# Attention stage of a decoder layer: score pieces of heads 0 and 1 made ahead, and later keys hidden on GpSimd after the exponential

## The chip, the core and the metric

The kernel runs on one NeuronCore of a Trainium2 chip. Its engines are TensorE (PE in the rows; PEld is its weight load), VectorE (DVE), ScalarE (ACT), GpSimd (POOL) and SyncE (SP, which issues DMAs). Each works through its own instructions in order and waits on semaphores for the others. The metric is the device time of one execution in microseconds (us); lower is better.

## What is computed

A decoder layer for 2048 tokens of 256 features: causal self-attention with 16 heads of 16 features, a second mixing step against a context of 1601 rows, and a feed-forward step with 8 experts, two of which are chosen for each token. The change touches the first of them, which the reference writes as

```
scores = jnp.einsum('bhqd,bhkd->bhqk', q, k) / jnp.sqrt(jnp.float32(Dh))
causal = jnp.tril(jnp.ones((S, S), dtype=bool))
scores = jnp.where(causal[None, None], scores, jnp.float32(-jnp.inf))
attn = jax.nn.softmax(scores, axis=-1)
out = jnp.einsum('bhqk,bhkd->bhqd', attn, v)
```

## The kernel before, in words

Three functions run one after the other: `project` (queries, keys, values, and the matrix of the second step), `attend` (the 16 heads) and `finish` (output products, second step, feed-forward step).

**Each head is computed twice over, in two layouts.** The softmax needs each query's highest score. So the scores are first made with the queries on the partitions, only to find their maximum: 35 **pieces** for a head (`PIECES`), most 512 columns wide. A piece is one product of `qstack` and `kstack` (`form_piece`, L154), and where it crosses the causal diagonal two more products with the matrix `hide_keys` (L161), which add -1e30 to later keys. VectorE takes a piece's maximum into `partial` (`reduce_piece`, L172). The letters of the pieces: w is 512 columns below the diagonal, d is 512 columns at it, n is 384 at it, p two of 256 and q four of 128. When all 35 are in, VectorE makes `neg_max` (L850), TensorE turns it (L807, the entry "max"), VectorE writes `max_row` (L855), and SP copies it by two DMAs into a row of `qstack` (L666), so that the scores of the second layout come out with the maximum taken off.

**The second layout** has the keys on the partitions, and goes by 10 **quads** for a head (`QUADS`): 512 queries against four tiles of 128 keys. Quads 0, 2, 5 and 9 of a head lie at the diagonal. For a quad `scores_half` makes two banks of scores (L747), ScalarE takes the exponential of each (L709) into one of three buffers `probs`, and `weigh` multiplies them by the values into `acc` (L774), two quads later (`LAG`). At the diagonal a score tile gets two more products, with `hide_queries` (L756), 64 and 128 columns wide, which again add -1e30. ScalarE copies `acc` out for each block of queries (L714), and the sums are folded (L782, "fold") and turned (L789, "turn").

**What sets the order.** TensorE's order in `attend` is a table, `PLACES`: for each of a head's 10 quads what goes behind the first half of the scores, behind the second half, and behind the weighing. What stands there are pieces of later heads and the entries fold, turn and max; they pass through a ring of three PSUM banks, which VectorE empties in the same order. During head h TensorE makes the pieces of head h+1 in quads 0 to 5 and those of head h+2 in quads 6 to 9: 35 in each of heads 0 to 13, 20 in head 14, none in head 15. In `project` another table (`pieces_behind`) puts pieces in pairs behind other products: all 35 of head 0 and the 15 early ones of head 1, 50 in all. `project` has three stretches that matter here: "v" (L552, 16 steps), "t" (L565, 13 steps) and "m" (L574, 26 steps).

**GpSimd** in `attend` prepares the weights of the third step: for each head it scales a load (L684), casts it (L687) and makes the rest (L689), all three in a row, after the load has landed. SP issues the max rows, the stacks of a head four ahead (12 DMAs), the store of the split weights and the next load, in this order.

## Time and profile before

| | us |
|---|---|
| Median of 3 runs | 839.01 (837.18 to 839.31) |
| The profiled execution, its own time | 840.59 |
| Its span, first to last instruction | 838.9 |
| `project`, from the start of the span to about | 88 |
| `attend`, about | 88 to 470 |
| `finish` | the rest |

| Engine | busy, us | share of the span |
|---|---|---|
| TensorE | 783.6 | 93% |
| VectorE | 559.2 | 67% |
| ScalarE | 512.3 | 61% |
| GpSimd | 303.8 | 36% |

The shares are averages over stages with different limits. In `attend`, VectorE is at nine tenths or more of nearly every slice, and falls to a third in `finish`. TensorE's granted clock is full nearly everywhere. Matmul ends are modelled, so for TensorE starts are a better measure than durations.

### The profile page before, as it was taken

To read this page: it belongs to the slowest core of one execution; us is meant where nothing else is said; L and a number is where in the kernel's file an instruction comes from. 1 tells how busy PE (TensorE), PEld (TensorE's weight loads), DVE (VectorE), ACT (ScalarE), POOL (GpSimd) and SP (SyncE) were. 2 spreads that over 40 slices of the span, in tenths; PEclk is the share of its full clock that TensorE was granted. 3 is DMA by queue.
4 is the path that set the end of the run, shared out by engine and by line. 5 is a ranking of instruction groups with operands and counts; after the bars stand their busy time and mean duration, and the time that the engine had idled before them with its cause. 6 is when DMAs were issued, how large, how long until landed. Compare 5 with 4: busy or idle time off the path is not lost. (4 is left out here: it accounts for less than half of the span.)

```text
span 838.9 us, 19596 instructions
## 1 busy us (share of the span) xinstructions
PE 783.6 (93%) x7434; PEld 496.9 (59%) x7435; DVE 559.2 (67%) x1072; ACT 512.3 (61%) x756; POOL 303.8 (36%) x226
## 2 busy tenths in 40 slices
PE   5899899999999999999998797889999999999994
PEld 1367344444443444444433585778888888877883
DVE  4575699999999999999980496973333333222395
ACT  4441687778887877788879487254444444343543
POOL 5040595555333355554550112132333333301121
PEclk9999799999999999999999999999999999999998
DMA  8783343334444443334232598452222222221362
GB/s 295 131 214 152 113 152 108 103 123 133 143 151 152 152 132 109 105 133 139 106 115 114 209 398 214 150 190 65 77 75 75 75 75 75 76 58 52 102 195 76
DMA packets 68362, 111.47 MB, mean 133 GB/s; under 512 B 39485, under 2 KB 49918, under 8 KB 63934
## 3 DMA queue, kind: packets, MB, share of 16 engines
q1 hardware_dynamic: 63134, 93.36, 35.7%
q0 software_dynamic: 4816, 16.65, 6.0%
q10 hardware_dynamic: 336, 0.40, 0.4%
q8 instruction: 54, 0.88, 0.4%
q14 instruction: 22, 0.18, 0.1%
HBM read 66.60 MB, written 32.37 MB: 118 GB/s over the span
## 5 line engine op out<-in xcount | busy, mean ns | idle before, releaser
L172 DVE TENSOR_REDUCE partial<-ring 128x1 f32<-128x512 f32 (+3 forms) x510 | 312.8, 670 | 24.2 <-PE ring L154 18.8
L709 ACT ACTIVATE probs<-scores 128x1024 f32<-128x1024 f32 (+1 forms) x320 | 270.5, 902 | 69.6 <-PE scores L747 36.9
L1284 ACT ACTIVATE hid<-turned 128x512 f32<-128x512 f32 (+1 forms) x112 | 65.6, 586 | 160.7 <-PE turned L1445 130.9
L154 PE MATMUL ring<-kstack,qstack 48*128 48x512 f16 (+1 forms) x581 | 156.4, 354 | 2.4 <-DVE partial L172 0.2
L774 PE MATMUL acc<-probs,values 128*32 128x512 f32 (+2 forms) x1472 | 156.6, 496 | 0.5 <-ACT acc_sb L714 0.3
L1470 PE MATMUL ops<-weights,work 128*128 (+1 forms) x1320 | 148.9, 273 | 2.7 <-DVE work L1685 1.4
L1445 PE MATMUL turned<-mats,weights 128*128 128x256 f16 (+1 forms) x1344 | 143.6, 262 | 3.2 <-DMA mats<-attn 2.2
L747 PE MATMUL scores<-qstack,kstack 49*128 49x512 f16 (+3 forms) x640 | 135.1, 352 | 7.2 <-ACT probs L709 5.9
L1685 DVE TENSOR_TENSOR work<-hid,work 128x512 f16<-128x512 f32 (+1 forms) x112 | 76.8, 690 | 94.9 <-ACT work L1289 94.8
L1470 PEld LDWEIGHTS ops<-weights,work 128*128 128x128 f16 x1320 | 128.4, 98 | 18.9 <-issue 3.8
L684 POOL TENSOR_TENSOR a_w_in<-a_w_in,w_scale 128x2304 f32<-128x2304 f32 x16 | 64.4, 4027 | 202.6 <-DMA a_w_in<-w_all 202.6
L1445 PEld LDWEIGHTS turned<-mats,weights 128*128 (+1 forms) x1344 | 122.2, 98 | 21.4 <-issue 4.4
L154 PEld LDWEIGHTS ring<-kstack,qstack 48*128 48x128 f16 x581 | 45.3, 94 | 116.5 <-DVE partial L172 101.5
L1209 POOL DMA_INDIRECT by_token<-attn,dest_u x39 | 38.7, 991 | 143.9 <-DVE attn L1694 138.1
L689 POOL TENSOR_TENSOR a_w_out<-a_w_in,a_w_out 128x2304 f16<-128x2304 f32 x16 | 73.0, 4566 | 1.3
L1289 ACT ACTIVATE work<-hid 128x512 f16<-128x512 f32 (+1 forms) x112 | 69.7, 622 | 4.7
L774 PEld LDWEIGHTS acc<-probs,values 128*32 128x32 f32 x1472 | 43.7, 109 | 36.8 <-issue 26.6
L747 PEld LDWEIGHTS scores<-qstack,kstack 49*128 49x128 f16 x640 | 40.6, 94 | 37.7 <-ACT probs L709 28.9
L1694 DVE COPY attn<-ops 128x512 f32<-128x512 f32 (+1 forms) x20 | 13.6, 678 | 68.8 <-PE ops L1470 68.8
L161 PEld LDWEIGHTS ring<-hide_keys,ident 64*128 64x128 bf16 x460 | 41.3, 95 | 17.3 <-issue 0.6
L161 PE MATMUL ring<-hide_keys,ident 64*128 64x128 bf16 x460 | 51.2, 203 | 0.0
L1201 POOL DMA_INDIRECT attn<-rows_d,token_u x39 | 38.1, 976 | 30.3 <-issue 10.7
(203 smaller groups left out, 742.5 us busy)
## 6 DMA issues: line engine op xcount, KB each, us to landing
a_w_in<-w_all SPq DMA_DIRECT2D x16, 1152.0 KB, 9.1
w_split_d<-a_w_out SPq DMA_DIRECT2D x16, 1152.0 KB, 5.7
weights<-w_split_d SPq DMA_DIRECT2D x6, 2048.0 KB, 19.8
weights<-w_split_d POOLq DMA_DIRECT2D x3, 2048.0 KB, 12.1
qstack<-q_split SPq DMA_DIRECT2D x72, 64.0 KB, 2.7
kstack<-k_split SPq DMA_DIRECT2D x72, 64.0 KB, 2.8
weights<-by_token SPq DMA_DIRECT2D x8, 512.0 KB, 7.6
attn<-xT SPq DMA_DIRECT2D x4, 512.0 KB, 7.4
```

Source lines behind the costliest of these rows:

```text
L154: mm = nc.tensor.matmul(bank[:, at:at + w], qstack[rows, slot, t * P:(t + 1) * P], kstack[rows, slot, c:c + w], start=True, stop=not diagonal)
L161: mm = nc.tensor.matmul(bank[:, at - P + a:at - P + b], ident16[rows, copy], hide_keys[rows, copy, a:b], start=False, stop=part == 1)
L172: return nc.vector.tensor_reduce(out=found[:, places[0]:places[-1] + 1:step], in_=bank[:, 0:WIDTH[n]].rearrange("p (k w) -> p k w", k=len( ...
L689: nc.gpsimd.tensor_tensor(w_out[:, h % 2, 1], w_in[:, h % 2], w_out[:, h % 2, 0], ALU.subtract).then_inc(w_lo, 1)
L709: nc.scalar.activation(probs[:, quad % NPROBS, at:at + w], scores[half][:, first:first + w], ACT.Exp, scale=QK_SCALE).then_inc(exp_done, 1)
L747: mm = nc.tensor.matmul(scores[half][:, at:at + w], kstack[used, slot, kt * P:(kt + 1) * P], qstack[used, slot, (qb + 1) * QB - w:(qb + 1) ...
L774: mm = nc.tensor.matmul(acc[VW * group:VW * (group + 1), first_query:first_query + w], values[:, h, k0 + j], probs[:, quad % NPROBS, at:at ...
L1284: nc.scalar.activation(h32, hps[b].rearrange("p (j n) -> p j n", n=TW)[:, :, 0:w], ACT.Silu, scale=1.0 / WSCALE).then_inc(silu_done, 1)
L1289: nc.scalar.activation(hid[:, parity, 0, b * HB:(b + 1) * HB, 0:w], h32, ACT.Copy).then_inc(hid_hi, 1)
L1445: mm = nc.tensor.matmul(place.rearrange("p (g n) -> p g n", n=P), weights[:, a, bass.ds(at + (k * HID + (b * HB + j) * P), P)], turned_row ...
L1470: mm = nc.tensor.matmul(bank[:, i], hid[:, parity, a, j, i * P:(i + 1) * P], weights[:, c, bass.ds(at + (WE // 2 + j * D), D)], start=(m = ...
L1685: nc.vector.tensor_tensor(hid[:, parity, 1, chunks, 0:w], hid32[:, b % 2].rearrange("p (j n) -> p j n", n=TW)[:, :, 0:w], hid[:, parity, 0 ...
```

## The change

1. **Pieces.** All 35 pieces of heads 0 and 1 are made in `project`, 70 in all, by putting a pair behind each step of "t" (before, behind two of three) and behind every second step of "m" (before, every fourth) but the last. The 490 others are dealt over `attend` by `deal_ring`, one head after the other, without regard to where a head begins: 34 in each of heads 0 to 2, 33 in each of heads 3 to 13, 25 in head 14. Within a head they stand more evenly: quad 1 and quad 8 hold one fewer than before.
2. **The entry "max"** no longer stands in quad 8, but four pieces behind the last piece of its head, so it moves from head to head: quad 1 in head 1, quad 2 in head 2, up to quad 8 in heads 12, 13 and 14. In head 13 it stands at the very end of quad 8, behind the weighing. For head 1 it is the first entry of `attend`.
3. **Later keys.** The products with `hide_queries` are gone, and so is the matrix. Instead GpSimd sets the probabilities of later keys to 0 behind the exponential: one `affine_select` for each half of a quad at the diagonal, over two blocks of 128 columns, 8 for a head. The weighing of such a quad now waits for `later_hidden`.
4. **GpSimd's weights.** The three steps for a head's weights are spread between the selects: two behind those of quad 5, and the third behind those of quad 0 of the next head.

```diff
-PLACES = (("", "wd", "w"), ("w", "w", "nw"), ("", "ww", "w"), ("d", "w", "w"), ("", "ww", "Fwp"),
-          ("", "wn", "w"), ("w", "d", "w"), ("w", "n", "w"), ("qMT", "wd", "nw"), ("", "ww", "wp"))
+ORDER = "wdwwnwqwdnwwwwpwdwwwnwwwwdwwwwwpwnw"
+PLACES = (("", "xx", "x"), ("x", "x", "x"), ("", "xx", "x"), ("x", "x", "x"), ("", "xx", "Fxx"),
+          ("", "xx", "x"), ("x", "x", "x"), ("x", "x", "x"), ("T", "xx", "xx"), ("", "xx", "xx"))
...
     if kind == "m":
-        return 2 if n % 4 == 3 else 0
-    return 2 * {"qk": n >= NQ * 4 - 2, "v": n % 2, "t": n % 3 != 2}[kind]
+        return 2 if n % 2 == 1 and n < DC * CT - 1 else 0
+    return 2 * {"qk": n >= NQ * 4 - 2, "v": n % 2, "t": 1}[kind]
...
+            def hide_later(h, qb):
+                quad = h * NQUAD + LAST_QUAD[qb]
+                for half in range(2):
+                    (_, a, _), (_, b, _) = halves_of(LAST_QUAD[qb])[half]
+                    at = half * 2 * QB + a
+                    pool.wait_ge(exp_done, 2 * quad + half + 1)
+                    blocks = probs[:, quad % NPROBS, at:at + 2 * (b - a)].rearrange("p (k n) -> p k n", k=2)[:, :, 0:P]
+                    nc.gpsimd.affine_select(out=blocks, in_=blocks, compare_op=ALU.is_ge, fill=0.0,
+                                            base=0, pattern=[[0, 2], [1, P]], channel_multiplier=-1).then_inc(later_hidden, 1)
...
             for h in range(H):
...
+                for qb in range(NQ):
+                    hide_later(h, qb)
+                    for _ in range(WEIGHTS_BEHIND[qb]):
+                        u = done // 3
+                        if done < 3 * H and (u < h or u == h and h > 0 or qb == 2):
+                            split_weights(u, done % 3)
+                            done += 1
...
-                if diagonal:
-                    for part, b in enumerate((GROUP, P)):
-                        for group, (j, at, w) in enumerate(halves_of(s)[half]):
-                            copy, used = hide_half(group, part), group_rows(group, GROUP)
-                            mm = nc.tensor.matmul(scores[half][:, at:at + b], ident16[used, copy],
-                                                  hide_queries[used, copy, 0:b], start=False, stop=part == 1)
...
             def weigh(h, s):
...
-                pe.wait_ge(exp_done, 2 * quad + 2)
                 first, last = k0 == 0, s == LAST_QUAD[qb]
+                if last:
+                    pe.wait_ge(later_hidden, 2 * (h * NQ + qb) + 2)
+                else:
+                    pe.wait_ge(exp_done, 2 * quad + 2)
```

**TensorE in `project`, the first five steps of "t".** A row is a line of the kernel, what it does, the tiles and the columns. Before:

```order
L565 MATMUL vt_ps0<-lm_sb,ctxT_sb 128x256 x2
L154 MATMUL piece_ps2<-kstack,qstack 128x512
L154 MATMUL piece_ps0<-kstack,qstack 128x512
L565 MATMUL vt_ps1<-lm_sb,ctxT_sb 128x256 x2
L154 MATMUL piece_ps1<-kstack,qstack 128x512
L154 MATMUL piece_ps2<-kstack,qstack 128x512
L565 MATMUL vt_ps0<-lm_sb,ctxT_sb 128x256 x2
L565 MATMUL vt_ps1<-lm_sb,ctxT_sb 128x256 x2
L154 MATMUL piece_ps0<-kstack,qstack 128x512
L154 MATMUL piece_ps1<-kstack,qstack 128x512
L565 MATMUL vt_ps0<-lm_sb,ctxT_sb 128x256 x2
```

And now (line 180 is the former line 154, line 585 the former 565):

```order
L585 MATMUL vt_ps0<-lm_sb,ctxT_sb 128x256 x2
L180 MATMUL piece_ps2<-kstack,qstack 128x512
L180 MATMUL piece_ps0<-kstack,qstack 128x512
L585 MATMUL vt_ps1<-lm_sb,ctxT_sb 128x256 x2
L180 MATMUL piece_ps1<-kstack,qstack 128x512
L180 MATMUL piece_ps2<-kstack,qstack 128x512
L585 MATMUL vt_ps0<-lm_sb,ctxT_sb 128x256 x2
L180 MATMUL piece_ps0<-kstack,qstack 128x512
L180 MATMUL piece_ps1<-kstack,qstack 128x512
L585 MATMUL vt_ps1<-lm_sb,ctxT_sb 128x256 x2
L180 MATMUL piece_ps2<-kstack,qstack 128x512
```

A pair now stands behind every step, where before every third step had none.

**TensorE in `attend`, a quad at the diagonal** (the last quad of the last head, which has no pieces around it). Before:

```order
L747 MATMUL scores0<-qstack,kstack 128x512
L747 MATMUL scores0<-qstack,kstack 128x128
L756 MATMUL scores0<-hide_queries,ident16 128x64 x2
L756 MATMUL scores0<-hide_queries,ident16 128x128 x2
L747 MATMUL scores1<-qstack,kstack 128x384
L747 MATMUL scores1<-qstack,kstack 128x256
L756 MATMUL scores1<-hide_queries,ident16 128x64 x2
L756 MATMUL scores1<-hide_queries,ident16 128x128 x2
L774 MATMUL acc<-probs,values 32x512 x8
```

And now:

```order
L792 MATMUL scores0<-qstack,kstack 128x512
L792 MATMUL scores0<-qstack,kstack 128x128
L792 MATMUL scores1<-qstack,kstack 128x384
L792 MATMUL scores1<-qstack,kstack 128x256
L812 MATMUL acc<-probs,values 32x512 x8
```

Eight small products have gone from the quad, and with them the place between the two halves' scores.

**GpSimd in `attend`, in the middle of the heads.** Before, the three steps for one head's weights stand in a row, and nothing lies between them:

```order
L694 TENSOR_TENSOR res<-res,bo_rows 128x1024 x4
L684 TENSOR_TENSOR a_w_in<-a_w_in,w_scale 128x2304
L687 CAST a_w_out<-a_w_in 128x2304
L689 TENSOR_TENSOR a_w_out<-a_w_in,a_w_out 128x2304
L684 TENSOR_TENSOR a_w_in<-a_w_in,w_scale 128x2304
```

And now, where `x4` are the selects of two quads:

```order
L709 AFFINE_SELECT probs<-probs 128x2x128 x4
L715 TENSOR_TENSOR a_w_in<-a_w_in,w_scale 128x2304
L721 CAST a_w_out<-a_w_in 128x2304
L709 AFFINE_SELECT probs<-probs 128x2x128 x4
L724 TENSOR_TENSOR a_w_out<-a_w_in,a_w_out 128x2304
L709 AFFINE_SELECT probs<-probs 128x2x128 x4
```

The last step (L689 before, L724 now) has moved between the selects of quad 0 and those of quad 2 of the next head.

## Rows read from the trace of the kernel before

**Rows 1.** The page's first part: busy time of each engine
```profile
PE 783.6 (93%) x7434; PEld 496.9 (59%) x7435; DVE 559.2 (67%) x1072; ACT 512.3 (61%) x756; POOL 303.8 (36%) x226
```

**Rows 2.** Windows: busy us (instructions), an ordinary head, then head 15
```profile
core 0: us, PE busy (x) PEld busy (x) DVE busy (x) ACT busy (x) POOL busy (x), PEclk, DMA share, GB/s
...
253.90:277.60 23.70, 23.35 (x256) 10.11 (x252) 22.36 (x40) 18.99 (x25) 10.59 (x4) 1.00 0.42 135
444.72:464.50 19.78, 17.58 (x187) 6.77 (x187) 0.68 (x2) 18.70 (x25) 0.00 (x0) 1.00 0.24 95
```

**Rows 3.** Timeline of VectorE in one head: start, length, what, count [idle before]
```profile
276.77 12.36 DVE L172 TENSOR_REDUCE partial<-ring 128x1 f32<-128x512 f32 x20
...
291.96 2.35 DVE L172 TENSOR_REDUCE partial<-ring 128x1 f32<-128x512 f32 x4 [0.57 <-PE ring L154]
```

**Rows 4.** Waits in one head, 270.3 to 293.95 us: total, times, longest
```profile
PEld ring L154 <- DVE partial L172: 7.0, 10, 0.8
...
DVE partial L172 <- PE ring L154: 0.9, 3, 0.6
```

**Rows 5.** TensorE's waits in head 15, 444.72 to 464.50 us
```profile
PE scores L747 <- ACT probs L709: 1.5, 5, 0.4
```

**Rows 6.** Timeline of TensorE in head 15, quads without pieces
```profile
446.38 0.64 PE L747 MATMUL scores<-qstack,kstack 49*128 49x512 f16 x4
446.94 0.75 PE L774 MATMUL acc<-probs,values 128*32 128x320 f32 x12
...
454.89 0.39 PE L747 MATMUL scores<-qstack,kstack 49*128 49x512 f16 x2
...
455.55 1.06 PE L774 MATMUL acc<-probs,values 128*32 128x512 f32 x8
```

**Rows 7.** Timeline of TensorE in the first stage, stretch "t"
```profile
53.89 1.13 PE L565 MATMUL vt_ps<-lm_sb,ctxT_sb 128*128 128x256 f32 x4
...
55.27 1.13 PE L565 MATMUL vt_ps<-lm_sb,ctxT_sb 128*128 128x256 f32 x4
...
56.94 2.00 PE L565 MATMUL vt_ps<-lm_sb,ctxT_sb 128*128 128x256 f32 x8
58.87 0.39 PE L154 MATMUL piece_ps<-kstack,qstack 48*128 48x512 f16 x2
```

**Rows 8.** The entry "max" on TensorE: shortest/median/longest ns, first and last start
```profile
L807 PE MATMUL ring<-ident,neg_max x15: 277/277/278, 109.1 to 440.5; 128*16 128x128 f32 x15
```

**Rows 9.** Windows at the start of the attention stage, columns as in rows 2
```profile
91.00:92.00 1.00, 0.82 (x11) 0.44 (x8) 1.00 (x3) 1.00 (x2) 0.00 (x0) 0.54 1.06 442
...
98.00:99.00 1.00, 1.00 (x8) 0.00 (x0) 0.00 (x0) 0.19 (x1) 1.00 (x1) 0.50 0.00 0
```

**Rows 10.** GpSimd's groups by line: count, busy us, mean ns, idle before
```profile
L443 POOL TENSOR_TENSOR values<-values,bv_rows 128x256 f32<-128x256 f32 x16 | 11.2, 721 | 29.3 <-ACT values L387 29.3
...
L420 POOL TENSOR_SCALAR_AFFINE_SELECT ident<-ident 128x128 f32<-128x128 f32 x1 | 0.3, 287 | 0.0
```

**Rows 11.** Timeline of GpSimd in one head, the longest step
```profile
276.50 4.57 POOL L689 TENSOR_TENSOR a_w_out<-a_w_in,a_w_out 128x2304 f16<-128x2304 f32 x1
```

**Rows 12.** Timeline of ScalarE: the exponentials of quads 0 and 2
```profile
280.99 1.30 ACT L709 ACTIVATE probs<-scores 128x640 f32<-128x640 f32 x2 [1.24 <-PE scores L756]
...
285.56 1.32 ACT L709 ACTIVATE probs<-scores 128x640 f32<-128x640 f32 x2
```

**Rows 13.** Timeline of TensorE: "max" turned, next head's first scores, weighing of quad 2
```profile
275.20 0.28 PE L807 MATMUL ring<-ident,neg_max 128*16 128x128 f32 x1
...
280.27 0.22 PE L747 MATMUL scores<-qstack,kstack 49*128 49x128 f16 x1
...
289.99 0.75 PE L774 MATMUL acc<-probs,values 128*32 128x320 f32 x12
```

**Rows 14.** Timeline of SyncE's queue: the DMAs of the max row are issued
```profile
276.21 1.15 SPq L666 DMA_DIRECT2D qstack<-max_row  x2
```

**Rows 15.** The tile `max_row`: from a DMA's issue to its landing
```profile
DMA to landing us min/median/max: 1.7/2.2/3.4
```

140 lines of the change are left out of this document (80 added, 60 removed).

## The prediction, made before the changed kernel ran

> **What bounds the kernel now.** I read the page's busy times first. TensorE is at 93% of the span, the others far below [rows 1], but that is an average over three stages, and the change lies in the first two. So I went on with windows. In an ordinary head of 23.7 us TensorE is busy for 23.35 us and VectorE for 22.36, ScalarE for 18.99, GpSimd for 10.59 [rows 2]. Two engines are nearly full at once, and the reader should see how they share the bound. VectorE's timeline shows 20 maxima without a gap in 12.36 us, 0.618 us each, and later short gaps that end with a piece from TensorE [rows 3]. The waits of one head say the same: VectorE waits 0.9 us for TensorE's pieces in a whole head, and TensorE's weight load for pieces is held by VectorE ten times [rows 4]. Most of that held time runs beside other products, since TensorE itself is idle for only 0.35 us. In head 15 no pieces are left. There the head takes 19.78 us, TensorE is busy for 17.58, and its stops are for ScalarE [rows 2, 5]. So pieces and masks are work on the bound in heads 0 to 14, and ScalarE sets a floor of about 19.8 us.
>
> From the two windows, a piece costs TensorE (23.35 - 17.58) / 35 = 0.165 us in `attend`, because it fills the idle row group beside the scores, and it costs VectorE 0.618 us.
>
> **Twenty pieces into the first stage.** They go as ten pairs. A step of "t" with its pair takes 55.27 - 53.89 = 1.38 us from start to start, and two steps without a pair between them 58.87 - 56.94 = 1.93, that is 0.97 for one [rows 7]. So a pair costs 0.41 us there, more than twice 0.165, since it stands alone between full-array products. Ten pairs are 4.1 us. Of the 20 pieces, 15 are w, 2 d, 2 n and 1 p, so six places at the diagonal come with them; each mask is 192 columns, which at the rate of the plain pair (512 columns in each of two row groups in about 0.3 us) is near 0.1 us: 0.6 us more. Sum 4.7 us, all on the path, because TensorE is what ends in this stretch. VectorE needs 2 x 0.618 = 1.24 us for a pair and has 1.38, so it keeps up, with 0.14 us to spare in each step. If that cover is gone, each step costs what VectorE lacks.
>
> **Fewer and more even pieces in the heads.** VectorE's part of a head with 35 pieces is 35 x 0.618 = 21.6 us and 1.1 us for the reciprocal, the product, the row and the last maximum: 22.7, and the rest to 23.7 is 1.0 us of gaps. With 33 pieces it is 20.4 + 1.1 + 1.0 = 22.5; with 34, 23.1.
>
> **The masks of the scores.** They are 16 x 4 x 8 = 512 small products. A quad at the diagonal without pieces takes 455.55 - 454.89 = 0.66 us with its masks, and a whole quad, which has more columns of scores (1024 against 896 in the fuller row group), 446.94 - 446.38 = 0.56 us [rows 6]. So the masks cost at least 0.10 us a quad, 0.4 a head. From above: they also keep the second row group idle until the first has finished, and pieces could fill that; 0.25 us a quad, 1.0 a head, is the most that I find in the columns. I take 0.7, since most quads have pieces to put there. TensorE's part of a head with 33 pieces is then 17.58 - 0.7 + 33 x 0.165 = 22.3 us and 0.35 idle: 22.65. Both engines come out within 0.15 us of each other, and I take 22.6: **1.1 us less** for each of heads 3 to 13. With 34 pieces VectorE sets 23.1, 0.6 less for each of heads 0 to 2. Head 15 is set by ScalarE and gains nothing. Head 14 has 5 pieces more than before (0.8 us of TensorE) and no masks (0.7): nothing.
>
> **The selects on GpSimd.** They lie between an exponential and the weighing, so what hides them is the two quads of lag. The trace has one select of 128 columns of f32 at 0.287 us; a sum of two tensors of 256 columns takes 0.721 us [rows 10]. The new one has 256 columns and one input, so 0.29 is its lower bound and 0.72 its upper, and I take 0.45, nearer to the row of its own kind. The tightest place is quad 2, since the longest step for the weights, 4.57 us [rows 11], now stands before it. The exponential of quad 0 ends at 280.99 + 1.30 = 282.29, and the weighing of quad 2 starts at 289.99 [rows 12, 13]: 7.7 us, and 7.3 when the head is 5% shorter. In this time GpSimd does a select, the long step and two selects: 4.57 + 3 x 0.45 = 5.9 us, and 6.7 at the upper bound. It fits with 1.4 us to spare, so I cost the selects at nothing. Queued behind a late select would be the other weight steps, and for it waits TensorE's weighing, with everything behind that. The three steps are also late in their turn by a few us, which only SP's store waits for, and that DMA has no reader before the last stage. The page gives GpSimd 36% [rows 1], so 128 selects of 0.45 us are no load.
>
> The Trainium skill, GPSIMD Engine Reference, section 3.1, states that data-dependent branching costs about 12 cycles an element; if a select were such work, 256 elements would be an estimated 2.6 us each by that page, and the sum would turn to slower, as in the second rival below. By that rule the 128 columns in rows 10 would have taken about 1.3 us; the trace has 0.287 and doesn't agree, so the sum goes by the row.
>
> **The entry "max".** In most heads it comes earlier than before and nobody waits for it. Before, TensorE turned it at 275.20 and needed the row at 280.27, 5.1 us later [rows 13]; SP issued the DMAs at 276.21 and they land about 2.2 us after the issue of the second, near 279 [rows 14, 15]. For head 14 it now stands behind the weighing of quad 8, about 2.4 us ahead of head 14's first scores (two pieces, then quad 9). The chain needs about 3.4 us there, as VectorE has little queued. So head 14 starts **1.0 us** late.
>
> **The sum.** -3 x 0.6 - 11 x 1.1 + 1.0 + 4.7 = -8.2 us. The profiled execution took 840.59 us for a span of 838.9, 1.6 us above the median of 839.01. I take the difference from the median: 830.8 us.
>
> **The rivals.**
>
> *More from the masks.* If they hold up the pairing of row groups in nearly every quad at the diagonal, and VectorE's gaps shrink with the more even table, a head gains 1.6 us: -3 x 1.2 - 11 x 1.6 + 5.7 = -15.5, 823.5 us. For it: eight products stand between the halves. Against it: VectorE at 21.5 us without gaps leaves little more.
>
> *Slower: selects that TensorE waits for.* One mechanism: at quad 2 of heads 3 to 15, GpSimd must finish the 4.57 us step and three selects in 7.3 us. It decides from (7.3 - 4.57) / 3 = 0.91 us a select. At 1.5 us each the weighing is 1.8 us late in each of 13 heads: +23 us, 854 us. Against it are both rows of rows 10; for it, that no row shows this form (two blocks, in place) and that spans on GpSimd are rough.
>
> *The gain meets another bound.* ScalarE has 18.99 us of 23.7 and no slack from quad 2 to quad 5, where copies lie between its exponentials. If heads gain only 0.4 us: -14 x 0.4 + 5.7 = +0.1, so 839 us, no change. VectorE's evenness argues against it.
>
> *The clock.* In head 0 TensorE's granted clock is at half (1.2 GHz of 2.4) from about 91.5 us on, after a stop between the two stages [rows 9]. From the first entry "max", at 109.1 us, to the one in rows 13 are seven heads, 23.7 us each [rows 8, 13]: so head 0 is the one that lost, about 2 to 3 us. If more pieces in "m" keep the clock up, the time is 828; if a stretch at half clock falls elsewhere, 834. This moves the forecast and turns no sign.
>
> *It doesn't do what it says.* The number of pieces is 560 in both tables, so 20 are moved and none saved; the masks of the pieces (L161) stay. That is as costed.
>
> **Chances.** The forecast with either clock (826 to 836) 0.60; more from the masks 0.15; another bound, no change 0.14; selects waited for 0.07; others that make it slower, such as VectorE falling behind in the first stage by more than 0.3 us a step, 0.04. The range reaches to the rivals at 823.5 and 839 with the clock's 3 us below: 820 to 838.5. Runs of this kernel differ by about 0.3%, 2.5 us, and what lies within that of 839 counts as no change: faster is then under 836.5, and gets 0.76, no change 0.14, slower 0.10.
>
> **What the profile of the changed kernel would show.** The first stage ends about 4.7 us later, with "t" and "m" steps of 1.38 us. From entry to entry of the reciprocal, an ordinary head takes 22.6 us. Selects take 0.3 to 0.7 us, and no wait of the weighing for `probs` from GpSimd stands among the waits. TensorE stops for about 1 us before head 14. VectorE still has stretches of 20 maxima without a gap; if they are gone and TensorE has no stops, the masks were worth more than 0.7. The prediction is wrong if selects take over 0.9 us, or if ScalarE's exponentials stand without gaps through a whole head.

## The result

| | before | after |
|---|---|---|
| Median, us | 838.94 (837.18 to 839.31, 4 runs) | 846.38 (845.62 to 848.25, 4 runs) |
| The profiled execution, us | 840.59 | 846.47 |
| Its span, us | 838.9 | 844.7 |
| Ratio to before | | 1.0096, 95% interval 1.0075 to 1.0118 |

The changed kernel is 7.4 us slower. The prediction was 830.8 us, with a range of 820 to 838.5: wrong in sign, and outside the range.

**Where the time went.** The stages are cut at starts that both traces have. First the start of the scores of head 0, of before and then of after, from TensorE's timeline:

```profile
87.99 0.37 PE L747 MATMUL scores<-qstack,kstack 49*128 49x512 f16 x2 [1.09 <-PEq L267]
```
```profile
92.63 0.37 PE L792 MATMUL scores<-qstack,kstack 49*128 49x512 f16 x2 [0.94 <-PEq L292]
```

Then the reciprocals, one for each head. The first, the thirteenth and the last of before, and the same three of after, from VectorE's timelines:

```profile
133.64 0.26 DVE L836 RECIPROCAL inv<-ring 128x16 f32<-128x16 f32 x1
...
418.63 0.26 DVE L836 RECIPROCAL inv<-ring 128x16 f32<-128x16 f32 x1
...
469.34 0.26 DVE L836 RECIPROCAL inv<-ring 128x16 f32<-128x16 f32 x1 [7.61 <-PE ring L789]
```
```profile
136.94 0.26 DVE L873 RECIPROCAL inv<-ring 128x16 f32<-128x16 f32 x1
...
423.07 0.25 DVE L873 RECIPROCAL inv<-ring 128x16 f32<-128x16 f32 x1
...
474.55 0.26 DVE L873 RECIPROCAL inv<-ring 128x16 f32<-128x16 f32 x1 [7.60 <-PE ring L827]
```

Twelve ordinary heads took (418.63 - 133.64) / 12 = 23.75 us each before and (423.07 - 136.94) / 12 = 23.84 after. The forecast had them 1.1 us shorter. With the first weighings of heads 1, 14 and 15 as further cuts (119.59, 428.33 and 449.42 us before; 123.42, 432.95 and 454.74 after) the spans split so:

| Stretch | forecast, us | measured, us |
|---|---|---|
| first stage | +4.7 | +4.6 |
| head 0, from its first scores | -0.6 | -0.8 |
| heads 1 to 13 | -13.3 | +0.8 |
| head 14 | +1.0 | +0.7 |
| head 15 up to the last reciprocal | 0 | -0.1 |
| `finish` | 0 | +0.6 |
| sum (difference of the two spans) | -8.2 | +5.8 |

Nearly all of the miss lies in the ordinary heads. The term of head 14 came near its size by another mechanism (see the account of the prediction), and head 0 begins at half clock in both kernels, so its -0.8 can't be put down to the pieces alone. The medians lie 7.4 us apart, the two profiled executions 5.9: the one of before took 840.59 us against a median of 838.94.

**The page after.** The first line corresponds to [rows 1]; the two groups are the maxima of the pieces on VectorE and the pieces on TensorE (columns: busy us, mean ns, idle us just before them with what ended most of it).

```profile
PE 781.0 (92%) x6922; PEld 478.7 (57%) x6923; DVE 562.0 (67%) x1072; ACT 512.5 (61%) x756; POOL 352.0 (42%) x350
...
L198 DVE TENSOR_REDUCE partial<-ring 128x1 f32<-128x512 f32 (+3 forms) x490 | 302.3, 669 | 35.1 <-PE ring L180 19.5
...
L180 PE MATMUL ring<-kstack,qstack 48*128 48x512 f16 (+3 forms) x560 | 154.2, 355 | 9.7 <-DVE partial L198 7.2
```

The same groups of before:

```profile
L172 DVE TENSOR_REDUCE partial<-ring 128x1 f32<-128x512 f32 (+3 forms) x510 | 312.8, 670 | 24.2 <-PE ring L154 18.8
...
L154 PE MATMUL ring<-kstack,qstack 48*128 48x512 f16 (+1 forms) x581 | 156.4, 354 | 2.4 <-DVE partial L172 0.2
```

TensorE has 512 products less and VectorE 20 maxima less in the heads, and both now wait for each other: VectorE's idle time before maxima grew by 10.9 us, TensorE's before pieces by 7.3. The windows of an ordinary head and of head 15, to be read against [rows 2]:

```profile
core 0: us, PE busy (x) PEld busy (x) DVE busy (x) ACT busy (x) POOL busy (x), PEclk, DMA share, GB/s
213.80:237.60 23.80, 22.77 (x219) 8.72 (x219) 21.74 (x39) 19.55 (x26) 13.78 (x11) 1.00 0.42 136
448.00:466.80 18.80, 16.57 (x151) 5.16 (x147) 0.57 (x3) 17.85 (x25) 7.69 (x9) 1.00 0.31 127
```

TensorE's work fell by 0.6 us a head and VectorE's by 0.6 [rows 2], and the head did not get shorter. In TensorE's timeline after, the waits stand where four pieces come together (over one head's length; idle before and its releaser in brackets):

```profile
237.42 0.39 PE L180 MATMUL ring<-kstack,qstack 48*128 48x512 f16 x1 [0.31 <-DVE partial L198]
...
261.15 0.39 PE L180 MATMUL ring<-kstack,qstack 48*128 48x512 f16 x1 [0.40 <-DVE partial L198]
```

Both stand in the turn of quad 0 (turns are explained next), and another wait of 0.30 us stands at 258.66 in that of quad 9. The reader should see that TensorE stops there for VectorE, though VectorE has 2 us to spare in the head as a whole.

### The profile page after: what moved, and what is told of

The parts are those of the page before. It is cut to its first block and busy times, and to the rows that moved or that the text cites. A ratio compares the mean times of both kernels' runs of the same rounds, so it can differ in the third digit from the quotient of the medians.

```text
span 844.7 us, 18690 instructions
## 1 busy us (share of the span) xinstructions
PE 781.0 (92%) x6922; PEld 478.7 (57%) x6923; DVE 562.0 (67%) x1072; ACT 512.5 (61%) x756; POOL 352.0 (42%) x350
## 5 line engine op out<-in xcount | busy, mean ns | idle before, releaser
L198 DVE TENSOR_REDUCE partial<-ring 128x1 f32<-128x512 f32 (+3 forms) x490 | 302.3, 669 | 35.1 <-PE ring L180 19.5
L180 PE MATMUL ring<-kstack,qstack 48*128 48x512 f16 (+3 forms) x560 | 154.2, 355 | 9.7 <-DVE partial L198 7.2
L1485 PE MATMUL turned<-mats,weights 128*128 128x256 f16 (+1 forms) x1344 | 145.5, 263 | 1.0 <-issue 0.7
L792 PE MATMUL scores<-qstack,kstack 49*128 49x512 f16 (+3 forms) x640 | 129.1, 352 | 9.4 <-ACT probs L755 7.2
L709 POOL TENSOR_SCALAR_AFFINE_SELECT probs<-probs 128x256 f32<-128x256 f32 x128 | 51.3, 407 | 184.4 <-ACT probs L755 184.4
L180 PEld LDWEIGHTS ring<-kstack,qstack 48*128 48x128 f16 x560 | 42.4, 94 | 128.0 <-DVE partial L198 111.4
L724 POOL TENSOR_TENSOR a_w_out<-a_w_in,a_w_out 128x2304 f16<-128x2304 f32 x16 | 73.1, 4567 | 0.1
L792 PEld LDWEIGHTS scores<-qstack,kstack 49*128 49x128 f16 x640 | 37.3, 94 | 41.6 <-ACT probs L755 31.2
```

Source lines behind the costliest of these rows:

```text
L180: mm = nc.tensor.matmul(bank[:, at:at + w], qstack[rows, slot, t * P:(t + 1) * P], kstack[rows, slot, c:c + w], start=True, stop=not diagonal)
L198: return nc.vector.tensor_reduce(out=found[:, places[0]:places[-1] + 1:step], in_=bank[:, 0:WIDTH[n]].rearrange("p (k w) -> p k w", k=len( ...
L724: nc.gpsimd.tensor_tensor(w_out[:, u % 2, 1], w_in[:, u % 2], w_out[:, u % 2, 0], ALU.subtract).then_inc(w_lo, 1)
L792: nc.tensor.matmul(scores[half][:, at:at + w], kstack[used, slot, kt * P:(kt + 1) * P], qstack[used, slot, (qb + 1) * QB - w:(qb + 1) * QB ...
L1485: mm = nc.tensor.matmul(place.rearrange("p (g n) -> p g n", n=P), weights[:, a, bass.ds(at + (k * HID + (b * HB + j) * P), P)], turned_row ...
```

## How the experiments are read: turns

The head's time is cut into ten **turns**. A turn of quad s runs from one weighing on TensorE to the next, and holds what stands behind the weighing in quad s - 1 and then both halves of quad s. Starts of weighings are read from TensorE's timeline; in all kernels but the changed one and its kin each head repeats them to 0.01 us. Pieces are counted from the table. Each ratio below is taken against the kernel before measured beside the run (medians 838.8 to 840.1 us). (The recorded expectations count quads from one: their "first quad" is quad 0, their "fourth" quad 3, their "seventh" quad 6, their "ninth" quad 8.)

| Turn of quad | 3 | 4 | 5 | 6 | 7 | 8 | 9 | 0 | 1 | 2 | head |
|---|---|---|---|---|---|---|---|---|---|---|---|
| pieces before | 3 | 3 | 4 | 3 | 3 | 4 | 4 | 4 | 3 | 4 | 35 |
| before | 2.04 | 2.11 | 3.07 | 2.27 | 2.01 | 3.07 | 2.39 | 2.58 | 1.97 | 2.25 | 23.75 |
| select_only | 2.04 | 2.11 | 3.06 | 2.28 | 2.01 | 3.06 | 2.39 | 2.58 | 1.97 | 2.25 | 23.75 |
| before_cheap | 2.04 | 2.12 | 2.85 | 2.27 | 2.01 | 2.88 | 2.19 | 2.36 | 1.97 | 2.25 | 22.94 |
| select_cheap | 2.04 | 2.12 | 2.85 | 2.28 | 2.00 | 2.88 | 2.19 | 2.31 | 1.97 | 2.25 | 22.89 |
| drop_bound | 2.04 | 2.11 | 3.07 | 2.27 | 2.01 | 3.07 | 2.39 | 2.13 | 2.18 | 2.09 | 23.35 |
| drop_slack | 2.25 | 1.93 | 3.06 | 2.27 | 2.01 | 3.07 | 2.39 | 2.58 | 1.97 | 2.25 | 23.77 |
| drop_lone | 2.04 | 2.12 | 3.06 | 2.05 | 2.19 | 3.06 | 2.39 | 2.58 | 1.97 | 2.25 | 23.70 |
| table_masks | 2.04 | 2.39 | 3.07 | 2.57 | 2.12 | 3.12 | 2.39 | 2.13 | 2.18 | 2.07 | 24.08 |
| table_select | 2.04 | 2.39 | 3.06 | 2.58 | 2.12 | 3.12 | 2.39 | 1.88 | 2.18 | 2.07 | 23.83 |
| one_moved | 2.04 | 2.49 | 3.06 | 2.27 | 2.01 | 3.07 | 2.39 | 1.88 | 2.18 | 2.08 | 23.47 |
| pair_s3 | 2.46 | 1.97 | 3.06 | 2.28 | 2.00 | 3.07 | 2.39 | 1.88 | 2.19 | 2.08 | 23.38 |
| pair_s6 | 2.04 | 2.11 | 3.06 | 2.58 | 2.12 | 3.12 | 2.39 | 1.88 | 2.19 | 2.08 | 23.57 |
| pieces after | 3 | 3 | 4 | 3 | 3 | 3 | 4 | 4 | 3 | 3 | 33 |
| after, head 5 | 1.99 | 2.61 | 3.03 | 1.97 | 2.29 | 2.34 | 2.39 | 2.49 | 1.97 | 2.25 | 23.33 |
| after, head 7 | 1.98 | 2.25 | 3.86 | 2.09 | 2.08 | 2.53 | 2.57 | 2.39 | 2.06 | 2.16 | 23.97 |

Two floors can be read off. Two exponentials of whole quads take ScalarE 1.94 to 1.99 us, and no turn of a whole quad is much shorter. Four maxima take VectorE 4 x 0.618 = 2.47 us [rows 3], and turns with four pieces lie at 2.25 to 2.6, as the ring lets a little of it spill into the next turn. Turns 5 and 8 are longer, since the fold stands in the one, and the last maximum, the turn of the sums and the piece of four parts in the other.

## First round: one part of the change at a time

**Selects alone.** The kernel before, with parts 3 and 4 of the change and its old table.

```
...
-                pe.wait_ge(exp_done, 2 * quad + 2)
+                if last:
+                    pe.wait_ge(later_hidden, 2 * (h * NQ + qb) + 2)
+                else:
+                    pe.wait_ge(exp_done, 2 * quad + 2)
...
```

> The kernel before with parts 3 and 4 of the change alone: the products with hide_queries are gone, GpSimd sets later keys' probabilities to 0, its weight steps stand between the selects; the table of pieces and the first stage are as before. Theory A (local bounds): quads 9 and 0 of a head hold four pieces each between two weighings, 4 x 0.618 = 2.47 us of VectorE, quads 2 and 5 end with ScalarE, so the masks lay beside a wait: 836 to 839 us, and the heads keep 23.7 us. Theory B (as predicted): the masks are 0.7 us of TensorE's bound in a head: 828 us, heads of 23.0 us; then the new dealing of the pieces must cost 18 us. By both, no weighing waits for GpSimd for more than 1 us in all.

Measured: 840.06 us (838.42 to 841.43), ratio 1.0010 (0.9998 to 1.0022). No turn moved by more than 0.01 us. Theory A was right on the heads; the total is 1 us above its range. The window of the same stretch as in [rows 2], and then TensorE's waits over 86 to 420 us (total, times, longest):

```profile
253.90:277.60 23.70, 22.82 (x220) 9.06 (x220) 22.36 (x40) 18.94 (x26) 13.81 (x11) 1.00 0.40 135
```
```profile
PE ring L155 <- DVE partial L173: 6.0, 26, 0.3
```

The same stretch and wait of before:

```profile
PE ring L154 <- DVE partial L172: 0.2, 1, 0.2
```

TensorE's busy time fell from 23.35 to 22.82, so the masks were indeed 0.53 us of its work in a head. All of it came back as waiting, 6.0 us of which the trace puts down to VectorE. Only head 15, which has no pieces, got shorter: reciprocal to reciprocal 19.35 us instead of 19.72, 0.37 less. That is close to the lower bound of the prediction (0.10 a quad).

**The dealing alone.** The kernel before with parts 1 and 2, and masks as products.

> The kernel before with parts 1 and 2 of the change alone: 70 pieces in the first stage, the rest dealt evenly, max four pieces behind; masks stay as products on TensorE. Theory A: the masks cost nothing in heads bound by VectorE and ScalarE, so this is as slow as the whole change, 845 to 848 us. Theory B: 846 + 11 = 857 us.

Measured: 847.56 us (845.61 to 851.34), ratio 1.0104 (1.0069 to 1.0140). This is theory A's range, and its heads 1 to 12 add up to within 0.3 us of those of the changed kernel. The whole loss lies in moving and dealing the pieces.

**The move without the new deal.** The old table, the maximum in its old place, all pieces two heads ahead and so 70 in the first stage; 35 a head, none in head 14.

```
...
-        kind, ahead = OTHERS[x] if x in OTHERS else ("piece", 2 if s in EARLY_QUADS else 1)
+        kind, ahead = OTHERS[x] if x in OTHERS else ("piece", 2)
...
```

> The kernel before with all 35 pieces of heads 0 and 1 in the first stage, but the old table: during each head all 35 pieces of the head two ahead, in the old places, and max in quad 8; none in heads 14 and 15. Masks stay. It isolates the move of 20 pieces. First stage +4.7 us, heads 0 to 13 as before at 23.75, head 14 at ScalarE's floor, 19.8 for 21.1: -1.3. Sum +3.4: 842.3 us. If the moved pieces were worth their 0.618 us of VectorE wherever they are taken out, -12.4 + 4.7: 831 us.

Measured: 844.23 us (843.86 to 847.50), ratio 1.0070 (1.0043 to 1.0096). Heads of 23.89 us, 0.14 more than before (0.12 of it in turn 1, and why isn't shown), and 20.66 instead of 22.66, reciprocal to reciprocal, for head 14, which has no pieces left. The total is 1.9 us above my 842.3. Each ordinary head still has its 35 pieces here, so the move alone makes none shorter: 4.6 us in the first stage are paid, and two come back in head 14.

**The maximum pinned.** The changed kernel with the entry of the last maximum always in quad 8.

```
-                if rows and (passed >= rows[0][1] + BEHIND or not left or rows[0][1] == 0):
+                if rows and (s, i) == (NQUAD - 2, 0):
```

> The changed kernel with the entry max put back into quad 8 ahead of turn, where it stood before; all else as changed. Theory A1: the drifting entry costs 0.25 to 0.9 us in most heads, since TensorE and VectorE stop for each other at it: 13 x 0.4 = 5 us less, 841 us, and the head with max in a fold quad loses its longer time. Theory A2: what costs is where the four-tile piece q and the other pieces with masks fall, and max is nothing: 845 to 847 us. Head 14 no longer starts 1.0 us late in both.

Measured: 845.33 us (844.14 to 846.60), ratio 1.0067 (1.0044 to 1.0090). Twelve heads of 23.65 us on average, against 23.84 with the moving maximum and 23.75 before. So the moving entry costs 0.2 us a head, less than theory A1 had. The total, in A2's range, shows only 1.0 us of it (2.4 by the two ratios). In the profiled executions pin_max is 4.15 us ahead of the changed kernel at the last reciprocal of `attend` (470.40 for 474.55) and 0.3 at the end: `finish` took 374.0 us instead of 370.1. Of these 3.9 us, 1.2 lie before its first reciprocal (13.64 us, against 12.46 in the changed kernel and 11.57 before); what makes the rest isn't shown. Where it hurts can be seen in head 7 of the changed kernel, where it falls behind the fold (TensorE's timeline):

```profile
270.66 1.05 PE L820 MATMUL ring<-acc_sb,fold 128*32 128x512 f32 x8
271.63 0.39 PE L180 MATMUL ring<-kstack,qstack 48*128 48x512 f16 x2
...
272.45 0.28 PE L847 MATMUL ring<-ident,neg_max 128*16 128x128 f32 x1 [0.21 <-ACT folded L767]
...
273.95 0.64 PE L812 MATMUL acc<-probs,values 128*32 128x512 f32 x4
```

Fold, two pieces, maximum and then the piece of four parts make this turn 3.86 us, against 3.07 before. With the maximum pinned it is still 3.40: 0.46 us is the maximum, and 0.33 stays with the other entries, among them the piece of four parts.

**The piece of four parts moves too.** It stood in turn 8 before; in the changed kernel and in pin_max it moves from head to head, since the pieces are dealt in one long row. The weighings around turn 4 of head 5, which ends with it, in pin_max and then in pinned_cheap (the same kernel with cheap maxima, below):

```profile
218.32 1.06 PE L812 MATMUL acc<-probs,values 128*32 128x512 f32 x8
...
220.93 0.75 PE L812 MATMUL acc<-probs,values 128*32 128x320 f32 x12
```
```profile
216.21 1.07 PE L812 MATMUL acc<-probs,values 128*32 128x512 f32 x8
...
218.85 0.75 PE L812 MATMUL acc<-probs,values 128*32 128x320 f32 x12
```

Turn 4 takes 2.61 us there, 2.64 with cheap maxima, and 2.11 before. The turn with this piece is long in other heads of pin_max too: 2.55 (turn 6, head 8), 2.48 and 2.58 (turn 7, heads 9 and 10), where before had 2.27 and 2.01. Cheap maxima leave these three at 2.55, 2.48 and 2.63, so VectorE doesn't set them. The piece is 12 small products on TensorE, four with two masks each. So pinning the maximum alone doesn't bring back the old head: theory A2 holds in part. No run moved this piece by itself.

The row at 271.63 above also shows two pieces of 512 columns in 0.39 us. The Trainium skill, TensorE: Matmul & The Clock Gate, section "Why this matters for your kernels", states that products with few rows run at the same time when each lies in a row group of its own; for this pair the trace agrees, since one such piece alone takes 0.39 us as well (237.42 above).

## Second round: what a lighter VectorE brings

**Cheap maxima, masks kept.**

```
-                                   in_=bank[:, 0:WIDTH[n]].rearrange("p (k w) -> p k w", k=len(places)), axis=X, op=ALU.max)
+                                   in_=bank[:, 0:WIDTH[n]].rearrange("p (k w) -> p k w", k=len(places))[:, :, 0:WIDTH[n] // len(places) // 2], axis=X, op=ALU.max)
```

> The kernel before, with masks as products and its old table, but each maximum of a piece reads only the first half of every block of its columns. The second half of the columns is left out of the row maxima, so the time is that of a kernel with a cheaper VectorE. An estimate of one such maximum is 0.35 us in place of 0.618, so VectorE's part of a head falls from about 22.7 to 13 us. Theory A (VectorE paces the quads at either end of a head, and TensorE's 23.35 busy us in a head of 23.7 are partly slow because it is held up): heads of 22.5 to 23.3, total 825 to 834. Theory C (TensorE's own work is the bound all along and VectorE only follows it): heads of 23.4 or more, total 835 to 838.

Measured: 825.55 us (822.98 to 828.24), ratio 0.9848 (0.9812 to 0.9884); heads of 22.94 us. Theory A was right, C fell.

**Cheap maxima, selects.** The same edit in select_only.

> As the run before this one (maxima over the first half of the columns alone; the rest of the columns is left out of the row maxima), with the products with masks taken out and the selects on GpSimd in. With the full maxima the selects were worth 0.0 us a head. Theory A (VectorE's queue hid the masks' time): now that VectorE is light, taking out the masks shows, 0.4 to 1.0 us a head, so 6 to 15 us less than the run before this one. Theory D (the masks run beside scores or pieces that TensorE executes anyway, and cost it nothing): within 2 us of the run before this one.

Measured: 826.71 us (824.87 to 829.78), ratio 0.9848 (0.9824 to 0.9872); heads of 22.89. One head of the first and one of the second, columns as in [rows 2]:

```profile
240.00:262.94 22.94, 22.73 (x258) 9.89 (x254) 14.05 (x40) 18.96 (x26) 10.74 (x4) 1.00 0.42 139
```
```profile
240.00:262.88 22.88, 22.31 (x224) 8.72 (x220) 13.92 (x40) 18.95 (x27) 13.79 (x11) 1.00 0.42 140
```

Two readings. VectorE's work fell by 8.3 us a head and the head by 0.8, in just four turns: 5, 8, 9 and 0, those with four pieces but turn 2. In the six others VectorE was never the bound. What holds turns 5 and 8 at 2.85 us and more then isn't shown. And the masks are worth 0.05 us even now, though TensorE does 0.42 us less. My theory A for this pair, that the masks would show once VectorE is light, fell; the rival D stands.

**A table with two pieces moved.** One piece each out of quads 0 and 1, one more each in quads 3 and 5; with masks and with selects.

```
-PLACES = (("", "wd", "w"), ("w", "w", "nw"), ("", "ww", "w"), ("d", "w", "w"), ("", "ww", "Fwp"),
-          ("", "wn", "w"), ...
+PLACES = (("", "d", "w"), ("w", "w", "w"), ("", "ww", "w"), ("d", "w", "nw"), ("", "ww", "Fwp"),
+          ("", "wn", "ww"), ...
```

> The kernel before with one change of its table: one piece less in the first quad and in the second, one more in the fourth and in the sixth. Masks stay products. Theory A (each quad is paced by the maxima of its own pieces, 0.618 us each, or by ScalarE): the quads that lose a piece shorten, those that get one had room on VectorE; with the masks, TensorE is nearly full too, so 0.0 to 0.5 us less a head, 831 to 839. Theory of the prediction (only the number of pieces in a head counts, and TensorE's sum): no change, 838 to 840.

Measured: 845.98 us (844.03 to 850.09), ratio 1.0094 (1.0065 to 1.0123); heads of 24.08.

> The same table as the run before this one, with the selects on GpSimd in place of the masks. Theory A (with pieces laid where VectorE has room, TensorE's sum is next, and the masks are then work on it): 0.5 to 0.8 us less a head than the kernel before, 827 to 833, and 3 us or more below the run before this one. Rival (ScalarE's chain, 19.9 us plus copies, or the ring of banks paces these quads): 836 to 840, and the same as the run before this one.

Measured: 842.53 us (841.73 to 846.57), ratio 1.0053 (1.0030 to 1.0077); heads of 23.83. Both were misses. Turn 0, with three pieces now, fell by 0.70 us with selects and by 0.45 with masks, but turns 4 and 6, with four now, rose by 0.28 and 0.31, and turns 7, 8 and 1 somewhat too. Beyond the heads, both kernels are 1.5 us behind before at the first reciprocal (135.16 and 135.24 us). It is the one place where the masks count: 0.25 us, in turn 0, once VectorE no longer paces it.

## Third round: what a piece is worth, and where

**Two pieces left out where VectorE paces** (one of quad 0, one of quad 8), and **two left out where it has room** (one of quad 2, one of quad 4).

```
-PLACES = (("", "wd", "w"), ... ("qMT", "wd", "nw"), ...
+PLACES = (("", "d", "w"), ... ("qMT", "d", "nw"), ...
```
```
-... ("", "ww", "w"), ("d", "w", "w"), ("", "ww", "Fwp"), ...
+... ("", "w", "w"), ("d", "w", "w"), ("", "w", "Fwp"), ...
```

> The kernel before (masks as products) with two pieces fewer in each head, out of the two quads that VectorE paces: one wide piece of the first quad and one of the ninth are not formed in any head, so their maxima are left out of the rows of maxima. With cheap maxima the intervals there fell from 3.07 to 2.88 and from 2.58 to 2.36 us, and with the table that takes one piece from the first quad the latter fell to 2.12. Theory A (a quad ends with the slowest of VectorE, ScalarE and TensorE in that quad): 0.4 us for each piece, 0.7 to 1.0 us a head, 826 to 830. Theory of the prediction (0.618 us of VectorE for a piece, up to TensorE's sum): 1.1 us a head or more, 824 or less.

> The kernel before with two pieces fewer in each head, out of two quads in which VectorE has room: one wide piece of the third quad and one of the fifth are not formed in any head, so their maxima are left out of the rows of maxima. Theory A: adding a piece to such a quad cost 0.28 to 0.31 us, taking one away gives 0 to 0.3 each, 0.2 to 0.5 us a head, 832 to 837, and less than in the run before this one. Theory of the prediction (only the count matters): as the run before this one, within 2 us.

Measured: drop_bound 834.82 us (834.20 to 837.23), ratio 0.9936 (0.9920 to 0.9953), heads of 23.35. drop_slack 842.50 us (840.33 to 843.93), ratio 1.0034 (1.0022 to 1.0047), heads of 23.77. Two pieces less brought 0.40 us a head in the one and nothing in the other. The weighings of drop_bound around turn 0, then those of drop_slack around turns 3 and 4:

```profile
250.95 1.06 PE L774 MATMUL acc<-probs,values 128*32 128x512 f32 x8
253.08 1.06 PE L774 MATMUL acc<-probs,values 128*32 128x512 f32 x8
255.27 0.75 PE L774 MATMUL acc<-probs,values 128*32 128x320 f32 x12
```
```profile
239.39 1.04 PE L773 MATMUL acc<-probs,values 128*32 128x512 f32 x8
241.65 1.06 PE L773 MATMUL acc<-probs,values 128*32 128x512 f32 x8
243.57 0.75 PE L773 MATMUL acc<-probs,values 128*32 128x320 f32 x12
```

In drop_bound turn 0 takes 2.13 and turn 1 2.19, where before had 2.58 and 1.97. In drop_slack turn 3 takes 2.26 and turn 4 1.92, where before had 2.04 and 2.11: what one turn gave, its neighbour took back. All 0.40 us of drop_bound come out of turns 0 to 2; the piece left out of quad 8 gave nothing. So a piece of 512 columns doesn't set turn 8. Without the piece of four parts, but with the maximum and three pieces, it takes 2.40 to 2.60 us in heads 1 to 10 of pin_max. Both forecasts for drop_bound's total, mine (826 to 830) and the one by the prediction's 0.618 us (824 or less), were too low, and so was mine for drop_slack (832 to 837): it does less work and is clear of before by 0.34%, on the slow side. The span of drop_slack is 1.6 us longer than that of before; 0.95 of it is there by the first reciprocal (134.59 us for 133.64), and what makes it was not tried.

**One piece moved within the head**, with the selects: from quad 0 behind the weighing of quad 3.

```
-PLACES = (("", "wd", "w"), ... ("d", "w", "w"), ...
+PLACES = (("", "d", "w"), ... ("d", "w", "ww"), ...
```

> The kernel before with the selects, and one piece moved within the head: out of the first quad (interval 2.58 us, paced by VectorE) into the third place of the fourth (interval 2.11 us, VectorE has room). Nothing is left out. Theory A, with the intervals of the run in which two pieces were moved: 0.5 to 0.7 us less around the first quad, 0.28 more in the fourth, so 0.2 to 0.4 us less a head, 834 to 837. Rival (every quad is as full as every other, as the run with two moved pieces had it): 839 to 842.

Measured: 836.00 us (835.44 to 837.66), ratio 0.9958 (0.9942 to 0.9975), heads of 23.47. Faster than both kernels, as expected.

**The changed kernel with a light VectorE**: pin_max with the cheap maxima.

> The changed kernel with the entry of the last maximum pinned to the ninth quad, and each maximum over the first half of each block of its columns alone (the rest is left out of the rows of maxima). It has 33 or 34 pieces a head in place of 35 and no masks. Theory A (VectorE light, a piece is then worth the 0.3 us of TensorE that adding one cost): 22.3 us a head, 0.5 less than with 35 pieces and selects, so with 4.6 us more in the first stage 822 to 827. Rival (ScalarE's chain is the floor and the pieces ride beside it): 22.8 a head as with 35 pieces, 830 to 833.

Measured: 831.24 us (830.12 to 836.16), ratio 0.9889 (0.9872 to 0.9905); twelve heads of 22.87 on average. This is what select_cheap has with 35 pieces. The rival held, my theory A fell: the change, with one or two pieces less a head, brings nothing even when VectorE is light. This pair of runs differs in the order of the pieces too, so it doesn't price a piece by itself.

## Fourth round: pieces that stand alone, pieces in pairs

A theory for what was left: since two pieces run at the same time in two row groups, the second of a pair would cost TensorE nothing and a lone one all of its columns.

> The kernel before with one piece fewer in each head: the wide piece of the first half of the seventh quad, which stands alone behind its scores, is not formed in any head, and its maxima are left out of the rows of maxima. Theory of pairs (a piece alone costs TensorE its 512 columns, the second of a pair costs nothing): the interval of 2.27 us there falls to 2.0, where ScalarE's two exponentials of 0.99 us are the floor, 0.27 us a head, 835 to 837, though only one piece is gone where two gone out of pairs gave nothing. Theory of slack (where VectorE has room a piece costs nothing): 23.75 a head, 838 to 841.

```
-... ("w", "d", "w"), ("w", "n", "w"), ...
+... ("", "d", "w"), ("w", "n", "w"), ...
```

Measured: 839.61 us (838.11 to 842.44), ratio 1.0004 (0.9989 to 1.0018), heads of 23.70: 0.05 less, not 0.27. ScalarE's timeline there in drop_lone, and then in before:

```profile
244.74 3.96 ACT L708 ACTIVATE probs<-scores 128x1024 f32<-128x1024 f32 x4 [1.10 <-PE scores L746]
```
```profile
247.23 1.94 ACT L709 ACTIVATE probs<-scores 128x1024 f32<-128x1024 f32 x2 [1.10 <-PE scores L747]
249.47 1.94 ACT L709 ACTIVATE probs<-scores 128x1024 f32<-128x1024 f32 x2 [0.30 <-PE scores L747]
```

Before, ScalarE had one gap of 0.30 us between quads 6 and 7, and the missing piece closed it: four exponentials now stand without a gap. Behind them the two kernels run alike, with the same 3.06 us in turn 8. ScalarE is the floor here, and 0.3 us was all that it left.

> The kernel before with the selects, and the piece from the first quad moved to the second half of the fourth, beside the wide piece that stands alone there (in one_moved it went behind the weighing and cost 0.38 us of an interval). Nothing is left out. Theory of pairs: TensorE executes it beside the other, so only VectorE's four maxima (4 x 0.618 = 2.47 us) can hold this interval of 2.04 us, and the ring's three banks even part of that out: 0.1 to 0.4 us more there, 0.5 less around the first quad, heads of 23.3 to 23.5, 832 to 837. Theory of slack alone: as one_moved, 23.47.

```
-PLACES = (("", "wd", "w"), ... ("d", "w", "w"), ...
+PLACES = (("", "d", "w"), ... ("d", "ww", "w"), ...
```

Measured: **834.05 us** (833.51 to 835.71), ratio 0.9945 (0.9926 to 0.9964), heads of 23.38. It leaves nothing out and is the fastest complete kernel of this study. The weighings of before and then of pair_s3, from turn 0 to turn 2 of one head:

```profile
255.29 1.06 PE L774 MATMUL acc<-probs,values 128*32 128x512 f32 x8
257.87 1.06 PE L774 MATMUL acc<-probs,values 128*32 128x512 f32 x8
259.84 0.75 PE L774 MATMUL acc<-probs,values 128*32 128x320 f32 x12
```
```profile
252.81 1.06 PE L786 MATMUL acc<-probs,values 128*32 128x512 f32 x8
254.69 1.06 PE L786 MATMUL acc<-probs,values 128*32 128x512 f32 x8
256.88 0.75 PE L786 MATMUL acc<-probs,values 128*32 128x320 f32 x12
```

Turn 0 went from 2.58 to 1.88 us, turn 1 from 1.97 to 2.19. The piece then makes turn 3 take 2.46, VectorE's four maxima (2.47), and leaves turn 4 at 1.97.

> The kernel before with the selects, and the piece from the first quad moved to the first half of the seventh, beside the wide piece that stands alone there; since the pieces of the seventh quad are formed two heads ahead, the first stage gets one more. Nothing is left out. Theory of pairs: that interval of 2.27 us has three maxima (1.85 us) and gets a fourth (2.47), TensorE's time does not grow: 0.1 to 0.2 us more there, 0.5 less around the first quad, heads of 23.2 to 23.4, and 0.3 us more in the first stage: 831 to 835. If a piece costs TensorE 0.3 wherever it stands: heads of 23.5, 836 to 838.

```
-PLACES = (("", "wd", "w"), ... ("w", "d", "w"), ...
+PLACES = (("", "d", "w"), ... ("ww", "d", "w"), ...
```

In quad 6 the pieces belong to the head after next, so the first stage gets one more. Measured: 838.47 us (835.14 to 840.39), ratio 0.9984 (0.9969 to 0.9999), heads of 23.57. Turn 6 rose by 0.31 us, as it had when the piece stood behind the weighing of quad 5 (table_select). So whether the piece has a partner made no difference: with drop_lone this refutes the theory of pairs. What differs between quads 3 and 6 is that turn 3 follows one with room and turn 6 follows turn 5, in which VectorE is behind. That explanation is argued, and wasn't tested by itself.

**The best table with the masks kept.**

> The table of pair_s3 (the piece from the first quad beside the one in the second half of the fourth) with the products with masks kept, no selects. Nothing is left out. Theory that VectorE's pace hid the masks in the first quad: the interval of 1.88 us there becomes 2.12, as it did between the two tables with two moved pieces, so 0.24 us more a head than pair_s3 and 0.37 more in the last head: 837 to 839. Rival (the masks are hidden wherever pieces stand): as pair_s3, 833 to 835.

Measured: 836.95 us (835.62 to 837.82), ratio 0.9975 (0.9966 to 0.9985), heads of 23.63: 0.25 us more than pair_s3, all in turn 0 (2.12 for 1.88), as expected. So the selects are worth something, but only beside a table that frees turn 0.

## Why the prediction was wrong, point by point

**The first stage: right.** The forecast was 1.38 us for a step of "t" with its pair and 4.7 us in all, from [rows 7]. After:

```profile
53.19 1.13 PE L585 MATMUL vt_ps<-lm_sb,ctxT_sb 128*128 128x256 f32 x4
54.26 0.39 PE L180 MATMUL piece_ps<-kstack,qstack 48*128 48x512 f16 x2
54.58 1.13 PE L585 MATMUL vt_ps<-lm_sb,ctxT_sb 128*128 128x256 f32 x4
```

54.58 - 53.19 = 1.39 us, and the stage ended 4.64 us later.

**The selects: right.** The forecast was 0.45 us each, hidden. After, the group (busy us, mean ns) and the only wait for one in the whole trace:

```profile
L709 POOL TENSOR_SCALAR_AFFINE_SELECT probs<-probs 128x256 f32<-128x256 f32 x128 | 51.3, 407 | 184.4 <-ACT probs L755 184.4
```
```profile
  POOL probs L709: 0.4, 1
```

0.407 us for two blocks of 128 columns lies between the bounds of [rows 10], 0.287 and 0.721. The Trainium skill, GPSIMD Engine Reference, section 3.1, gives about 12 cycles an element for data-dependent branching. The measured time speaks against taking a select for such work, as [rows 10] did.

**The entry "max" at head 14: the number near, the mechanism wrong.** Forecast: head 14 starts 1.0 us late, for its maximum row. In the trace TensorE has no wait for that row before head 14, whose first quad's turn takes 2.57 us as before. The 0.7 us lie in turn 8 of head 14, 3.20 us for 2.09, at the maximum of head 15, which stands right behind the last piece, so that TensorE waits for VectorE; turn 9 gives 0.62 back. After, from the timelines of TensorE and of its weight load:

```profile
446.54 0.27 PE L847 MATMUL ring<-ident,neg_max 128*16 128x128 f32 x1 [0.91 <-DVE neg_max L879]
```
```profile
450.21 0.23 PEld L792 LDWEIGHTS scores<-qstack,kstack 49*128 49x128 f16 x4 [1.04 <-DMA qstack<-max_row]
```

The one wait for a maximum row is that of head 15, 1.04 us of the weight load. Most of it lies beside the weighing from 449.02 to 450.09; the scores start at 450.22. So the term's size was luck.

That the entry moves through the other heads was costed at nothing ("nobody waits for it"). It was 0.2 us a head (pin_max). Its row never came late there; the clearest loss is where it stands in the turn with the fold.

**The masks, 0.7 us a head: the step that failed first.** The size on TensorE was roughly right, 0.53 us of busy time. The step from TensorE's busy time to the head's time was not: the sum took TensorE's 23.35 busy us of 23.7 [rows 2] for its own work, back to back. In the heads the freed time became waiting, most of it for VectorE (select_only). Measured: 0.0 us a head with the old table, 0.25 with turn 0 freed, 0.37 in the head without pieces.

**The pieces, 0.165 us of TensorE and 0.618 of VectorE each: the step that failed next.** Both are means over a head, used as if each piece cost its mean. Measured, a piece is worth what its turn says: 0.4 us in turn 0 (drop_bound), 0.05 in turn 6 (drop_lone), nothing in turn 8 (drop_bound) and in turns 2 and 4 (drop_slack). The change took one piece out of turn 2, which stayed at 2.25 us, and one out of turn 8, together with the maximum. Turn 8 fell from 3.07 to 2.34 (head 5), but, as far as drop_bound and pin_max show, less for the piece gone than for two entries that left it: the piece of four parts and the maximum, which now lengthen turns elsewhere. Turn 4 is 0.50 longer in head 5, with the maximum pinned as well, so that is the pieces in it; turn 5 is 0.79 longer in head 7, of which the maximum makes 0.46. The prediction had no term for where the piece of four parts stands. Turns 5, 9 and 0, with four pieces each, were left as they were: 3.03, 2.39 and 2.49. "More even" held for the count of pieces in a quad, not for the turns that VectorE paces.

**VectorE's gaps.** The prediction kept them at 1.0 us a head. They grew, though "more even" was to shrink them if anything: VectorE is busy 21.74 of 23.80 us after, so 2.06 idle, against 23.70 - 22.36 = 1.34 before. The longest stretch of maxima that I found without a gap has 14, not 20. I read this as gaps that three banks are too few to make up; no run tried another ring.

**The rivals.** "The gain meets another bound" was the nearest, with 839 us and a chance of 0.14. It named ScalarE. In before, ScalarE has no gap from 259.51 to 269.88 us, that is through turns 2 to 4, and one of 0.30 us between quads 6 and 7. The other bound is VectorE, which has a share in turns 5, 8, 9 and 0 (before_cheap). The rival's gain of 0.4 us a head was still too much: 0.09 were lost. Neither of the prediction's two signs of being wrong came: selects took 0.41 us, and ScalarE was busy for 19.55 of 23.80 us, with gaps. So both signs looked away from VectorE. The chances erred where they took TensorE's 93% as a sum to subtract from, while the same rows showed VectorE holding TensorE's weight load for 7.0 us in a head [rows 4]. The clock was as before at the start of `attend`. At the start of `finish` it cost 1.7 us in the first sixteen turns, 0.9 by the first reciprocal, less than the 3 that the rival allowed for.

**Which runs turned the sign.** select_only and deal_only: without the heads' gain, 4.6 us in the first stage are left as a loss. The heads' own loss (0.8), head 14 (0.7) and `finish` (0.6), less 0.8 in head 0, make the 5.8 of the two spans; the 7.4 of the medians hold run-to-run spread as well.

## What to carry to other kernels

When two or three engines are nearly full in a loop (here TensorE 98%, VectorE 94%, ScalarE 80%), cut the loop at fixed points of the order (here the weighings) and ask of each part which engine paces it: work taken off one engine is worth only the distance to the next engine in that part, and nothing elsewhere. A mean cost per item (busy time over count) should not enter a sum of savings; find the parts in which the item's queue is full and count the items there. One letter moved in the table, aimed at the fullest part, brought 0.25% alone (pair_masks) and 0.55% with the selects (pair_s3), where the whole change lost 0.96%. And an order that moves costly entries from head to head hides where they cost.
